# Values' products of two rounds in one visit of TensorE, and the sums of an attention divided anew between POOL and VectorE

## The chip, the cores and the metric

The kernel runs on one core of one Trainium2 chip. The metric is the device time of one execution in microseconds (us). TensorE is PE in the profile, with its weight loads as PEld; VectorE is DVE, ScalarE is ACT, GpSimd is POOL, SyncE is SP. A granted clock of 1.00 is TensorE at 2.4 GHz, its other level is 1.2 GHz.

## What is computed

Four blocks follow each other, each behind a layer norm and with a residual: a small state-space model, a feed-forward with quantized weights, an attention and a feed-forward with a mixture of low-rank parts. The change touches the third alone:

```python
q = jnp.dot(x, Wq).reshape(b, t, H, HD).transpose(0, 2, 1, 3)         # b 2, t 1024, H 32, HD 32
kv = jnp.dot(x, Wkv).reshape(b, t, G, 2, HD).transpose(2, 3, 0, 1, 4)  # G 8, four heads share k and v
scores = jnp.einsum('bhqd,bhkd->bhqk', q, k)
scores = jnp.where(causal[None, None], -jnp.inf, scores)
weights = jax.nn.softmax(scores * (1.0 / HD ** 0.5), axis=-1)
ctx = jnp.einsum('bhqk,bhkd->bhqd', weights, v)
return jnp.dot(ctx, Wo) + bo
```

All is float32. Where a plain matmul would not be exact enough, a factor is split into a high part (rounded to fp32r) and a low part (the rest), and three matmuls take the place of one.

## The kernel before

The attention is class `StageC`. Its loop has 16 **groups** `o` (two batches, eight sets of four heads `g` that share keys and values). A group has 12 **rounds** `r` (`ROUNDS`): rounds 0 to 3 are the first half of the queries (512 of them) against key blocks 0 to 3, rounds 4 to 11 the second half against key blocks 0 to 7. Rounds 0 to 3 and 8 to 11 touch the diagonal: they need a mask and have 512, 384, 256 and 128 columns; rounds 4 to 7 have 512. A round has four **slots**, one per head, so a group has 48 slots `s`, and `S = 48 * o + s` numbers them all. Each engine runs its own program over the same slots, and they meet in semaphores only.

**PE** (`pe`). Each slot has a score (`pe_score`, L2003: keys of one block against the queries of one head, into one of three PSUM banks) and one piece of the row maxima of the group ahead (`pe_amax`, L1985, in a ring of three other banks that `pe_turn` hands out). Many slots have a step of the projection of later query weights (`pe_job`, L1961 to L1963, three matmuls; in an ordinary group in even slots 2 to 16 and 32 to 46, so slots 18 to 31 have none). In slot 1 of a round (`g == 1`) comes a **visit** with the values' products (`pe_pv`, L2018) of the round two before: four heads side by side on 32 columns of the array each, two instructions per head, so eight matmuls in a row of the timeline. They accumulate in bank 5 over a half, and a half begins only when the half before has been copied out. `pe_sum` (L2044) makes the softmax denominators from the running sum `S` with a matrix of ones: at s == 5 for the second half of the group before, at s == 20 for the first half. In the groups `BY_ROUND` (4, 5, 14, 15) the first half's denominators are made round by round from the exponentials (`pe_sums`, L2034) inside the visit. `pe_mrow` transposes the maxima at s == 38.

**ACT** (`act_exp`, L2172). One exp per slot, from the score's bank into `P`, a ring of three rounds (`R % 3`, with R the round's number over all groups). The first head of round R waits until the products of round R - 3 are done, and the heads wait until the sums have read that buffer. ACT also casts the weights' high parts (`act_w4`, L2106) and the queries (`act_job`, L2130), and copies out the denominators and products of a half (`act_evac`, L2180 and L2185, at s == 6 and s == 22). In each slot the denominators' copy comes ahead of the exp, the products' copy behind it.

**DVE** (`dve`). One maximum per slot (`dve_amax`, L2323 and L2327), the low part of the queries (`dve_job`, L2312), the low parts of the next query weights in four pieces (`low_w4`, L2256), reciprocals, and in slots 23 to 26 the pair sums of rounds 4 and 5, one head each (`dve_pair`, L2269). At the end of the stage (`LAST`) it makes the running sums of groups 14 and 15 (`dve_last`, L2283).

**POOL** (`pool`). For each round, behind its last exp: the mask (`affine_select`, L2414), a multiplication of a finished half by its reciprocals (`pool_mul`, L2392, in rounds 0 and 4), and the running sum over rounds in `S` (round 1 in four instructions at L2431 and L2432, the others L2435; round 6 in two halves, L2408 and L2410). By the table `POOL_W` it also makes the low parts of a query weight in two places where the key weights' projection has crowded the slots: in round 8 of group 4 and in round 9 of group 8.

The order of work is written out by hand in the tables `JOBS`, `POOL_W`, `LAST`, `BY_ROUND` and in the fixed slots of each engine's loop. A semaphore that counts adds (`adds`, `psum_s`) tells how far `S` is.

## Time and profile before

| | |
|---|---|
| median of 3 runs | 2193.08 us (2185.26, 2194.05, 2193.08) |
| the profiled execution | 2189.54 us, span 2187.7 us, granted clock 0.969 |
| PE, DVE, ACT, POOL busy over the span | 2030.2, 1423.0, 946.4, 1003.7 us |
| attention: first score to last products | 957.7 to 1719 us |

The attention's groups take about 46.5 us each where nothing special happens (groups 1, 2, 7, 11, 12). "Busy" is the time in which an engine had an instruction under way; matmuls overlap, so 0.39 us for 512 columns is the life of one, and the distance of the starts is what it costs. A row of the windows view gives the stretch and its length, then the busy time (and number of instructions) of PE, the weight loads, DVE, ACT and POOL, the granted clock, the DMA engines' busy share and GB/s. A row of a timeline gives the start, the length, the engine, line, operation, result and operands, and how many such instructions it joins. An idle time in brackets names what ended it, by the semaphore that came last in the profile.

### The profile page before, as it was taken

Reading aid. Unit: us, or ns where it says so; the run is one execution under the profiler, and the core shown is the slowest. Engines: PE = TensorE matmul, PEld = TensorE weight load, DVE = VectorE, ACT = ScalarE, POOL = GpSimd, SP = SyncE. Lnnn points to the kernel's source line nnn. Section 1 sums busy time; section 2 is a strip of 40 time slices with the busy share of each in tenths; the row PEclk is TensorE's granted clock in tenths of the full one; section 3 lists DMA queues with packets and bytes.
Section 4 is the critical chain, followed back from the end, with each engine's and each line's share of the span. In section 5 each row is a group of like instructions: output and inputs, shape, how many; then the busy total and the mean of one; then the engine's idle time right before and its main releaser. Section 6 shows DMA issues by size and latency. Waiting matters only on the chain.

```text
span 2187.7 us, 30701 instructions
## 1 busy us (share of the span) xinstructions
PE 2030.2 (93%) x10444; PEld 1451.2 (66%) x10444; DVE 1423.0 (65%) x3290; ACT 946.4 (43%) x1979; POOL 1003.7 (46%) x866
## 2 busy tenths in 40 slices
PE   5889986999999989889999999999988999999998
PEld 4654545788888879755566555555554687888887
DVE  6877667677777762386765677567668577654433
ACT  5645685233333333135554555455555433332311
POOL 1444586544444430028875587667883133220000
PEclk9989998999999999999999999999997999999999
DMA  5400376122222147422223722323223375554332
GB/s 185 177 3 7 113 239 224 48 77 78 77 78 78 68 173 275 106 54 64 61 73 103 205 71 74 86 62 83 61 70 123 98 245 175 179 166 149 135 121 101
DMA packets 146475, 249.65 MB, mean 114 GB/s; under 512 B 27166, under 2 KB 77214, under 8 KB 146192
## 3 DMA queue, kind: packets, MB, share of 16 engines
q1 hardware_dynamic: 135312, 227.77, 32.8%
q10 hardware_dynamic: 11008, 19.93, 2.9%
q8 instruction: 83, 1.36, 0.3%
q14 instruction: 72, 0.59, 0.1%
HBM read 139.89 MB, written 76.02 MB: 99 GB/s over the span
## 4 chain that ended last, share of the span: by engine, by line
PE 60%; POOL 11%; DVE 9%; issue 3%; DMA 3%; ACT 2%; ACTq 1%; SPq 1%; DVEq 0%; POOLq 0%
POOL c_S L2435 7%; PE PS L2643 5%; PE PS L2644 5%; PE PS L2647 5%; PE PS L1130 3%; PE PS L1129 3%; PE PS L1128 3%; PE PS L2003 3%; PE PS L2018 3%; PE PS L1985 3%; PE PS L1178 2%; DVE PS L2327 2%; PE PS L1179 2%; PE PS L1180 2%; PE PS L1961 2%
## 5 line engine op out<-in xcount | busy, mean ns | idle before, releaser
L2172 ACT ACTIVATE c_P<-PS 128x512 f32<-128x512 f32 (+3 forms) x768 | 357.4, 494 | 320.6 <-PE PS L2003 301.4
L1985 PE MATMUL PS<-c_K,c_Q 96*128 96x512 f32 (+3 forms) x768 | 276.9, 371 | 21.3 <-DVE cst L2327 13.3
L2003 PE MATMUL PS<-c_Q,c_K 97*128 97x512 f32 (+3 forms) x768 | 282.5, 381 | 5.6 <-DMA c_Q<-c_mT 2.9
L2435 POOL TENSOR_TENSOR c_S<-c_S,c_P 128x2048 f32<-128x2048 f32 (+3 forms) x94 | 272.5, 2899 | 8.6 <-ACT c_P L2172 0.2
L2003 PEld LDWEIGHTS PS<-c_Q,c_K 97*128 97x128 f32 x768 | 147.8, 195 | 172.6 <-ACT c_P L2172 97.2
L2323 DVE TENSOR_REDUCE cst<-PS 128x1 f32<-128x512 f32 x256 | 175.9, 687 | 91.8 <-PE PS L1985 91.1
L213 POOL TENSOR_TENSOR maskw<-maskw,mhalf 128x1 f32<-128x1 f32 x64 | 37.1, 580 | 364.3 <-DVE maskw L171 351.9
L1985 PEld LDWEIGHTS PS<-c_K,c_Q 96*128 96x128 f32 x768 | 150.2, 196 | 77.0 <-DVE cst L2327 36.2
L2018 PE MATMUL PS<-c_P,c_V 128*32 128x512 f32 (+3 forms) x1536 | 168.5, 511 | 14.5 <-ACT c_P L2172 8.7
L2327 DVE CUSTOM_DVE_ANT_0 PS<-PS,maskw,cst 128x128 f32<-128x128 f32 (+3 forms) x256 | 142.9, 558 | 59.2 <-PE PS L1985 42.9
L2327 DVE CUSTOM_DVE_ANT_0 PS<-PS,maskw 128x128 f32<-128x128 f32 (+3 forms) x256 | 126.4, 504 | 62.6 <-PE PS L1985 60.5
L1274 ACT ACTIVATE b_g<-PS 128x460 f32<-128x460 f32 x96 | 53.0, 552 | 259.1 <-PE PS L1150 122.4
L1388 DVE SCALAR_TENSOR_TENSOR b_pr<-b_g,b_a 128x460 f32<-128x460 f32 x192 | 157.1, 854 | 1.7
L2414 POOL TENSOR_SCALAR_AFFINE_SELECT c_P<-c_P 128x512 f32<-128x512 f32 x128 | 83.0, 648 | 159.5 <-ACT c_P L2172 159.4
L1486 POOL TENSOR_TENSOR b_gp<-b_g 128x230 f32<-128x230 f32 x96 | 84.8, 883 | 152.1 <-DVE b_g L1373 152.1
L1128 PE MATMUL PS<-b_w13h,b_xsh 128*128 128x460 f32 (+1 forms) x384 | 148.1, 386 | 5.9 <-DVE b_xsl L1359 5.9
L2643 PE MATMUL PS<-c_xth,d_xh 128*128 128x512 f32 x376 | 147.7, 393 | 0.0
L2644 PE MATMUL PS<-c_xtl,d_xh 128*128 128x512 f32 x376 | 146.5, 390 | 0.0
L1130 PE MATMUL PS<-b_w13h,b_xsl 128*128 128x460 f32 (+1 forms) x384 | 143.8, 374 | 0.0
L1129 PE MATMUL PS<-b_w13l,b_xsh 128*128 128x460 f32 (+1 forms) x384 | 143.7, 374 | 0.0
L1961 PE MATMUL PS<-c_xth,c_wh 128*128 128x512 f32 x304 | 125.2, 412 | 5.5 <-POOL c_wl L2256 2.3
L1962 PE MATMUL PS<-c_xtl,c_wh 128*128 128x512 f32 x304 | 121.3, 399 | 0.0
(300 smaller groups left out, 4748.8 us busy)
## 6 DMA issues: line engine op xcount, KB each, us to landing
a_xin<-in_x SPq DMA_DIRECT2D x32, 512.0 KB, 4.4
d_x<-scr SPq DMA_DIRECT2D x32, 512.0 KB, 4.8
c_Q<-c_qh SPq DMA_DIRECT2D x240, 64.0 KB, 2.0
scr<-a_xin SPq DMA_DIRECT2D x16, 512.0 KB, 5.7
b_xn<-scr SPq DMA_DIRECT2D x16, 512.0 KB, 5.6
b_x<-scr SPq DMA_DIRECT2D x16, 512.0 KB, 4.8
scr<-b_x SPq DMA_DIRECT2D x16, 512.0 KB, 2.6
scr<-b_y SPq DMA_DIRECT2D x16, 512.0 KB, 3.0
```

Of the source, the lines that this page charges most:

```text
L1128: e.matmul(o, self.xsh[:, par, i, :], wh[:, v, i, :], start=i == 0 and not late, stop=False, skip_group_check=True)
L1129: e.matmul(o, self.xsh[:, par, i, :], wl[:, v, i, :], start=False, stop=False, skip_group_check=True)
L1130: m = e.matmul(o, self.xsl[:, par, i, :], wh[:, v, i, :], start=False, stop=i == 1 and bool(late), skip_group_check=True)
L1985: e.matmul(bank[:, 0:hi - lo], self.Q4[0:96, 4 * (o % 3) + g, 128 * t:128 * t + 128], self.K4[0:96, HEADS[o % 8], lo:hi], start=True, stop ...
L2003: e.matmul(self.k.bank(i % 3)[:, 0:hi - lo], self.K4[0:97, HEADS[o % 8], 128 * kt:128 * kt + 128], self.Q4[0:97, 4 * (o % 3) + g, lo:hi], ...
L2018: m = e.matmul(k.bank(5)[32 * g:32 * g + 32, lo - 512 * half:512], self.V[:, kt, o // 8, HEADS[o % 8], :], P[:, g, 0:hi - lo], start=kt == ...
L2172: e.activation(self.P[:, R % 3, g, 0:hi - lo], self.k.bank(i % 3)[:, 0:hi - lo], ACT.Exp, scale=SCALE).then_inc(self.exp_s.s, 1)
L2323: e.tensor_reduce(m, r, AX, ALU.max).then_inc(self.mx_s.s, 1)
L2327: e.tensor_tensor_reduce(out=r, in0=r, in1=self.maskw[:, 512 - n:512], scale=1.0, scalar=m if lo > 0 else -3.0e38, op0=ADD, op1=ALU.max, a ...
L2435: e.tensor_tensor(S[:, :, 512 - n:512], S[:, :, 512 - n:512], P[:, :, 0:n], ADD).then_inc(self.psum_s.s, 1)
L2643: e.matmul(o, h, wh[:, c, cols], start=c == 0, stop=False)
L2644: e.matmul(o, h, wl[:, c, cols], start=False, stop=False)
```

## The change

It has five parts, all in `StageC`.

1. In twelve groups (all but `SINGLE`: 5, 8, 14, 15) the values' products of rounds R - 1 and R run in one visit, in slot 1 of each odd round, and even rounds have no visit. The bank for the denominators by round (group 4) is taken at s == 13.
2. The denominators of the first half move from slot 20 to slot 21, behind the products; ACT copies them out behind the exp of slot 22, not ahead of it.
3. The low parts of the query weights go from DVE (slots 18 to 21) to POOL, round 4, in groups 1, 2, 3, 6, 7, 10, 11 and 12. In POOL's order they now stand behind the multiplication.
4. The pair sums of rounds 4 and 5: DVE makes heads 0 and 1 (slots 23 and 24), POOL heads 2 and 3 in one add in round 5.
5. Round 7 (`BOTH`): POOL adds heads 0 and 1, DVE heads 2 and 3 in slots 35 and 36 (not in groups 14 and 15). POOL's add of round 8 waits for DVE's.

```diff
+SINGLE = (5, 8, 14, 15)
-POOL_W = {(4, 8): JOB[7] + 1, (8, 9): JOB[11] + 1}
+POOL_W = {(4, 8): JOB[7] + 1, (8, 9): JOB[11] + 1} | {(o, 4): JOB[o + 3] + 1 for o in (1, 2, 3, 6, 7, 10, 11, 12)}
+BOTH = 7
...
-                if g == 1 and S > 8:
-                    self.pe_pv(e, *divmod(S // 4 - 2, 12))
+                R = S // 4 - 2
+                if g == 1 and R >= 0:
+                    if R // 12 in SINGLE:
+                        self.pe_pv(e, *divmod(R, 12))
+                    elif r % 2:
+                        self.pe_pv(e, *divmod(R - 1, 12))
+                        self.pe_pv(e, *divmod(R, 12))
                 if s == 5 and o > 0:
                     self.pe_sum(e, 2 * o - 1)
-                if s == 20 and o not in BY_ROUND:
+                if s == 21 and o not in BY_ROUND:
                     self.pe_sum(e, 2 * o)
...
             elif r3 in (4, 5):
-                e.wait_ge(*self.pair_s(4 * o3 + g + 1))
+                if g < 2:
+                    e.wait_ge(*self.pair_s(2 * o3 + g + 1))
+                elif g == 2:
+                    e.wait_ge(*self.pairp_s(o3 + 1))
...
+            elif r3 == BOTH and o3 < 15 and g == 2:
+                e.wait_ge(*self.both_s(2 * o3 + 2))
...
+                self.act_exp(e, o, r, g)
                 if s == 22:
                     self.act_evac(e, 2 * o, 1)
-                self.act_exp(e, o, r, g)
...
+    def dve_both(self, e, o, g):
+
+        e.wait_ge(*self.exp_s(48 * o + 4 * BOTH + g + 1))
+        e.wait_ge(*self.psum_s(self.adds(o, BOTH - 1)))
+        e.tensor_tensor(self.S[:, g, :], self.S[:, g, :], self.P[:, (12 * o + BOTH) % 3, g, :], ADD).then_inc(self.both_s.s, 1)
...
-                if 23 <= s < 27:
+                if 23 <= s < 25:
                     self.dve_pair(e, o, s - 23)
+                if s in (35, 36) and (o, BOTH) not in LAST and o < 15:
+                    self.dve_both(e, o, s - 33)
...
-                    e.wait_ge(*self.pair_s(4 * o + 4))
+                    e.wait_ge(*self.pair_s(2 * o + 2))
                     e.wait_ge(*self.exp_s(48 * o + 4 * r + 2))
                     e.tensor_tensor(S[:, 0:2, :], S[:, 0:2, :], P[:, 0:2, :], ADD)
+                    e.wait_ge(*self.pairp_s(o + 1))
...
+                if o > 0 and r in (0, 4):
+                    self.pool_mul(e, 2 * o - (2 if r == 0 else 1))
                 if (o, r) in POOL_W:
                     for q in range(4):
                         self.low_w4(e, POOL_W[o, r], q)
-                if o > 0 and r in (0, 4):
-                    self.pool_mul(e, 2 * o - (2 if r == 0 else 1))
+                if r == 5:
+                    e.wait_ge(*self.summed(2 * o - (o in BY_ROUND)))
+                    e.tensor_tensor(S[:, 2:4, :], self.P[:, (12 * o + 4) % 3, 2:4, :], P[:, 2:4, :], ADD).then_inc(self.pairp_s.s, 1)
...
                 e.wait_ge(*self.psum_s(self.adds(o, r - 1)))
-                e.tensor_tensor(S[:, :, 512 - n:512], S[:, :, 512 - n:512], P[:, :, 0:n], ADD).then_inc(self.psum_s.s, 1)
+                if r == BOTH + 1:
+                    e.wait_ge(*self.both_s(2 * o + 2))
+                gs = slice(0, 2 if r == BOTH else 4)
+                e.tensor_tensor(S[:, gs, 512 - n:512], S[:, gs, 512 - n:512], P[:, gs, 0:n], ADD).then_inc(self.psum_s.s, 1)
```

## Rows read from the trace of the kernel before

**Rows 1.** Busy time of the engines in the stretch of group 7, windows view.

```profile
1295.00:1342.00 47.00, 44.67 (x261) 27.27 (x261) 33.24 (x93) 26.49 (x61) 36.91 (x24) 1.00 0.27 69
```

**Rows 2.** Chain of waits over the same stretch, by engine, tile and line.

```profile
by line: POOL c_S L2435 42.1%; POOL c_S L2408 5.1%; POOL c_P L2414 5.1%; POOL c_S L2410 5.0%; DVE PS L2327 4.9%; PE PS L1985 4.8%; issue 4.7%; PE PS L2003 4.6%; DVE c_S L2269 4.2%; DVE cst L2323 3.8%; PE PS L2018 3.8%; PE PS L1961 3.1%; PE 
```

**Rows 3.** POOL's timeline from slot 20 of group 7 to slot 6 of group 8.

```profile
1315.33 1.34 POOL L2392 TENSOR_TENSOR c_cH<-c_cH,c_cS 128x512 f32<-128x512 f32 x1 [0.83 <-ACT c_P L2172]
1323.84 2.39 POOL L2408 TENSOR_TENSOR c_S<-c_S,c_P 128x1024 f32<-128x1024 f32 x1 [7.17 <-DVE c_S L2269]
...
1328.72 4.59 POOL L2435 TENSOR_TENSOR c_S<-c_S,c_P 128x2048 f32<-128x2048 f32 x1
...
1333.98 4.59 POOL L2435 TENSOR_TENSOR c_S<-c_S,c_P 128x2048 f32<-128x2048 f32 x1
...
1342.65 0.63 POOL L2414 TENSOR_SCALAR_AFFINE_SELECT c_P<-c_P 128x512 f32<-128x512 f32 x1
...
1346.43 1.28 POOL L2435 TENSOR_TENSOR c_S<-c_S,c_P 128x512 f32<-128x512 f32 x1
```

**Rows 4.** PE's timeline: slots 1, 5 and 45 of group 7.

```profile
1296.97 0.64 PE L2018 MATMUL PS<-c_P,c_V 128*32 128x256 f32 x8 [1.04 <-ACT c_P L2172]
...
1301.30 1.07 PE L2044 MATMUL PS<-c_S,cst 128*32 128x512 f32 x8 [0.22 <-POOL c_S L2435]
...
1339.30 0.85 PE L2018 MATMUL PS<-c_P,c_V 128*32 128x384 f32 x8 [0.24 <-POOL c_P L2414]
```

**Rows 5.** PE's timeline: slots 16, 17, 18, 20 and 32 of group 7.

```profile
1311.21 0.39 PE L2003 MATMUL PS<-c_Q,c_K 97*128 97x512 f32 x1
...
1312.37 0.40 PE L2003 MATMUL PS<-c_Q,c_K 97*128 97x512 f32 x1
1312.60 0.22 PE L1985 MATMUL PS<-c_K,c_Q 96*128 96x128 f32 x1
1312.76 0.64 PE L2018 MATMUL PS<-c_P,c_V 128*32 128x256 f32 x8
...
1313.67 0.40 PE L1985 MATMUL PS<-c_K,c_Q 96*128 96x512 f32 x1
...
1315.34 1.06 PE L2044 MATMUL PS<-c_S,cst 128*32 128x512 f32 x8 [0.45 <-DVE cst L2323]
...
1325.39 0.40 PE L2003 MATMUL PS<-c_Q,c_K 97*128 97x512 f32 x1
```

**Rows 6.** PE's timeline: products and denominators in one visit, group 4.

```profile
1149.78 1.06 PE L2018 MATMUL PS<-c_P,c_V 128*32 128x512 f32 x8
1150.66 1.04 PE L2034 MATMUL PS<-c_P,cst 128*32 128x512 f32 x8
```

**Rows 7.** ACT's timeline: exps of slots 19 and 23 to 25.

```profile
1314.65 0.60 ACT L2172 ACTIVATE c_P<-PS 128x512 f32<-128x512 f32 x1
...
1319.10 1.61 ACT L2172 ACTIVATE c_P<-PS 128x512 f32<-128x512 f32 x3
```

**Rows 8.** VectorE's timeline: two subtractions of low parts and a pair sum.

```profile
1315.11 0.41 DVE L2256 TENSOR_TENSOR c_wl<-c_raw,c_wh 128x256 fp32r<-128x256 f32 x1
...
1315.85 1.10 DVE L2256 TENSOR_TENSOR c_wl<-c_raw,c_wh 128x256 fp32r<-128x256 f32 x1
...
1320.18 0.69 DVE L2269 TENSOR_TENSOR c_S<-c_P 128x512 f32<-128x512 f32 x1
```

**Rows 9.** POOL's timeline: subtractions of low parts in group 4.

```profile
1184.29 2.79 POOL L2256 TENSOR_TENSOR c_wl<-c_raw,c_wh 128x256 fp32r<-128x256 f32 x4
```

**Rows 10.** POOL's timeline: a mask in group 14, while VectorE adds.

```profile
1679.52 0.98 POOL L2414 TENSOR_SCALAR_AFFINE_SELECT c_P<-c_P 128x512 f32<-128x512 f32 x1 [1.26 <-ACT c_P L2172]
```

**Rows 11.** Waits of attention: us in total, times, longest.

```profile
PE PS L1961 <- POOL c_wl L2256: 2.3, 2, 1.3
```

**Rows 12.** Windows view, slots 41 to 45 of group 13.

```profile
1630.00:1635.00 5.00, 3.67 (x16) 2.20 (x16) 2.47 (x6) 1.21 (x5) 5.00 (x2) 0.59 0.42 125
```

More of the change, by code:

```diff
@@ L1614, in __init__ @@
          self.whi_s, self.wlo_s, self.amax_s, self.mx_s, self.mtr_s, self.mtc_s, self.score_s, self.exp_s, self.diag_s,
-         self.pair_s, self.psum_s, self.pv_s, self.sum_s, self.evv_s, self.evs_s, self.rec_s, self.mul_s, self.wo_s) = k.sigs(
-            "c_", "given xtr xhi xlo vmm vcp qmm qhi qlo whi wlo amax mx mtr mtc score exp diag pair psum pv sum evv evs rec mul wo")
+         self.pair_s, self.psum_s, self.pv_s, self.sum_s, self.evv_s, self.evs_s, self.rec_s, self.mul_s, self.wo_s, self.both_s, self.pairp_s) = k.sigs(
+            "c_", "given xtr xhi xlo vmm vcp qmm qhi qlo whi wlo amax mx mtr mtc score exp diag pair psum pv sum evv evs rec mul wo both pairp")
         self.xld = [Sig(k, "c_x", 16, s, n) for s, n in ((before.ldc, 6), (before.ldb, 1), (before.lda, 1), (before.ld2, 6))]
@@ L1662, in tables @@
                     keeps.append(turn(o, 50))
-                if o in BY_ROUND and s == 9:
+                if o in BY_ROUND and s == (9 if o in SINGLE else 13):
                     kept = turn(o, 49)
@@ L1666, in tables @@
                     keeps.append(kept)
-                if o not in BY_ROUND and s == 20:
+                if o not in BY_ROUND and s == 21:
                     keeps.append(turn(o, 49))
@@ L2281, in dve_last @@
         else:
-            e.wait_ge(*(self.pair_s(60 + g + 1) if (o, r) == (15, 6) else self.dsum_s(n - 1, g)))
+            e.wait_ge(*((self.pair_s(30 + g + 1) if g < 2 else self.pairp_s(16)) if (o, r) == (15, 6) else self.dsum_s(n - 1, g)))
         e.tensor_tensor(self.S[:, g, cols], self.S[:, g, cols], self.P[:, (12 * o + r) % 3, g, 0:hi - lo], ADD
```

## The prediction

> **What bounds the kernel now.** I read the windows first, then the chain of waits, then the timelines of one attention group. In group 7 PE is busy 44.67 of 47 us, at the full 2.4 GHz, but POOL is busy 36.91 of 47 us as well [rows 1]. The chain over the same stretch lies on POOL's running sum for more than half of its length [rows 2]. The timeline of POOL shows how: from slot 20 on it waits 7.17 us for VectorE's last pair sum, and then it never stops, from 1323.84 to the end of the last add of the group at 1347.71 [rows 3]. PE runs into the tail of it: at slot 1 of each group the values' products wait 1.04 us for the mask of round 10, which stands behind an add on POOL (the trace names ACT), at slot 5 the denominators wait another 0.22 us for POOL's last add, and at slot 45 a mask costs 0.24 us [rows 4]. The first two come back in groups 2, 3, 7, 8, 11, 12 and 13 and in group 1. A third stall stands at slot 20, where the denominators of the first half wait 0.45 us for a PSUM bank [rows 5]. So the period of a group is one loop: denominators at slot 5 (1301.30), slot 16 (1311.21, 9.9 later), exps of round 5 and pair sums (12.6), POOL's chain (23.9), denominators at slot 5 of the next group (0.1 later): 46.5.
>
> **What the change does, part by part.** I write P16 for the start of slot 16.
>
> Visits. Twelve groups go from 12 visits with values' products to 6: 72 fewer. A visit costs more than its streaming. From the product at 1312.60 to the one at 1313.67 pass 1.07 us [rows 5]. In it lie 128 columns (0.06), a score (0.23, the spacing of 512 columns by 1312.37 to 1312.60) and products of 256 columns. Two sets of 512 columns in one visit start 0.88 us apart [rows 6], so 256 columns stream in 0.44. The rest, 0.3 us, is what entering and leaving costs. Bounds: 0 (if all of it belonged to the streaming) and 0.35. I take 0.3, the row that shows a visit. The denominators' move from slot 20 to 21 makes them share a visit too, and their bank has then been read, so 0.3 and 0.45 go, twelve times.
>
> Slots 16 to 31 take 14.18 us now [rows 5]. Without the stalls (some 2.0, the ones shown and smaller ones for VectorE) and with three visits fewer (0.9), PE would need 11.2. But ACT has work there: exps at 0.5 us each (three in 1.61 us, the last 0.6 long), two evacuations, a cast and four weight casts [rows 7]. I followed it: the exp of slot 23 ends 8.7 us after P16 (now 8.5), the next come every 0.5, and the score of slot 29, which needs the exp of slot 26, cannot start before 10.2. Then come a double visit of 2.3 with its products and two slots of 0.9 together: 13.4. Gain 0.8 of the 3.0 that PE alone would give.
>
> Late exps. In an odd round the first exp writes the buffer of three rounds before, whose products now run only in slot 1 of that round: it starts about 1.5 us later. PE has the second set (0.98), a score and a maximum (0.57) before it asks for that exp, and 0.7 more where the slot has query steps. The exp is 0.6 long and its start lags the end of the products by some 0.2. So 1.55 covers 0.8, and nothing waits. Cost zero; if the cover were one set shorter, 0.3 to 0.4 per visit.
>
> The weights' low parts. In 8 groups four subtractions leave VectorE (0.41 long each [rows 8]) and go to POOL in round 4 (four in 2.79 us [rows 9]). They fall into POOL's idle 7.17 us: the multiplication starts at P16 + 4.1 [rows 3], ends at 5.4, the subtractions end at 8.2. The one whose casts come last is ready at 6.7. The next load of weights on SP waits for them and is no later than now.
>
> Pair sums. Two of four leave VectorE (0.69 long each [rows 8]). POOL makes both in one add of 1024 columns, 2.4 us, and needs the exp of slot 23. That can start at P16 + 8.7. Then come the two adds of round 6 (4.9) as now.
>
> Round 7. POOL adds 1024 columns instead of 2048: 2.45 instead of 4.6. VectorE adds the other two heads in slots 35 and 36, and POOL's add of round 8 now waits for them.
>
> Loop for a group with all parts, ideal: pair sum at 8.7, + 2.45, + 4.9, + 2.45, + 1.15 (mask of round 8 and the wait for VectorE), + 13.7 (start of the add of round 8 to the end of round 11's, 1333.98 to 1347.71 [rows 3]) = 33.35. Now it is 12.63 + 23.87 = 36.5. Denominators 0.08 later, then 9.9 to the next P16, less one visit: 9.6. Period 43.0 against 46.5, a gain of 3.5. PE's own loop would be 42.6, so POOL still sets it.
>
> **A price that speaks against the change.** VectorE and POOL disturb each other. The subtraction on VectorE that took 0.41 us at 1315.11 took 1.10 at 1315.85 [rows 8]: it lay under POOL's multiplication (1315.33 to 1316.67 [rows 3]) and ended 0.28 after it. The other way round, a mask of 0.63 us took 0.98 where VectorE streamed sums [rows 10]. Neither starves the other, the one that waits gets the next turn. The change puts four additions of VectorE into stretches where POOL works. The first pair sum of VectorE (wanted at 7.05) meets the subtractions, the second too, and POOL's pair sum then starts at 9.4 instead of 8.7. In round 7 VectorE's two adds are wanted at 17.3 and 18.2, while POOL adds until 19; they end at 19.7 and 21 with the mask in between, and round 8 starts 1.9 instead of 1.15 after round 7. Loop: 9.4 + 2.45 + 4.9 + 2.45 + 1.9 + 13.7 = 34.8; period 44.5; gain 2.0 per group. I take this one, since the 1.10 us comes back in seven groups, and longer in two more. The Trainium skill (SBUF — State Buffer, Who interferes with whom) says that an instruction of VectorE with two SBUF inputs and one of GpSimd that reads SBUF exclude each other for the whole instruction. The trace agrees (1.10 against 0.41). Without such a rule the gain would be the 3.5 above.
>
> **The sum.** Nine loops (from groups 0, 1, 2, 3, 6, 7, 10, 11, 12) at 2.0: 18. Group 13 has no query steps after slot 31, so POOL alone sets it: in a stretch of it POOL is busy 5.00 of 5 us and PE 3.67 [rows 12]. By the same loop, with the start at 8.7 (nothing is subtracted in it), round 8 begins at 20.4 instead of 22.8; with two visits: 3. Groups 6 and 10, whose first slots PE bounds, one visit each: 0.6. Group 0 waits at slot 20 for POOL's add of round 3, and one slot of cover comes ahead of that: 1. Group 4: four visits and POOL's earlier turn on key weights, whose two stalls are 2.3 us [rows 11]: 2.4. Group 8: 1.7 (the other of these stalls and slot 20's). Group 5: two pair sums off a late VectorE, 1.3. Group 9: the same and visits, 2.1. Groups 14 and 15: 1.3. Together 31.4. The profiled execution took 2189.54 us, so it would take 2158; the median of the runs shown is 3.5 higher, so I forecast 2162.
>
> **Rivals.**
> A. No meetings of weight: 3.5 instead of 2.0 in nine loops (13.5), some 1.5 more in group 13: 2147. For it: VectorE has slack beside query steps. Against it: the 1.10. Chance 0.2.
> B. POOL's chain hardly starts earlier. If POOL's pair sum gets in ahead of VectorE's second one, that one ends 3 us later, and round 6 needs both; if also VectorE's adds of round 7 come behind the mask, round 8 starts 1 us later still. The gain per loop falls to about 0.5: 2175. It decides at 9.4 after P16. Chance 0.22.
> C. Slower: the late exps. If the exps of odd rounds come so late that PE waits 0.7 us in each of the 72 double visits, this costs 50 and eats the 31: 2212. It needs 0.44 us per visit to turn the sign, that is an exp that starts 1.2 us after its products, or products whose completion shows only after the second set. Against it: exps now follow products and scores within 0.5 us. Chance 0.07.
> D. The change doesn't do what its first part says: the 0.3 us belong to the streaming of these products and stay when two visits become one. POOL's loop then gains 1.7 instead of 2.0 (nine times), and the groups that PE bounds some 4 less in all: 2168. Chance 0.06.
> A fifth thing moves any of these: after the long stalls of group 13 the granted clock fell to 0.59 of full (a mean over both levels, 2.4 and 1.2 GHz) [rows 12]. Stalls that go may save such stretches, a new stall of that size may add one: 3 us either way.
>
> **How the numbers follow.** My forecast has 0.45, with its own range 2153 to 2171. A measurement of this kernel can tell about 0.5% (11 us) from no change. Faster by more, below 2182: forecast, A, D and half of B: 0.82. Within 0.5%: the other half of B, 0.11. Slower: C, 0.07. The range of 8 in 10 runs from 2142 (A, with the clock's part) to 2184 (B with a few more).
>
> **What would show it.** In the changed profile: the products on PE in rows of 16 and 6 visits a group; the exp of slot 28 about 1.5 us later than its score and no wait of PE for exps at slot 31; POOL's pair sum about 9.4 us after P16 and round 8's add about 21; VectorE's sums 1 to 2.4 us long where POOL works; the stall at slot 1 gone and one of 1 to 2 us before the denominators at slot 5; a period near 44.5 us in groups 1, 2, 7, 11, 12. I am wrong if POOL idles between rounds 5 and 11, if PE waits for ACT in the odd rounds, or if the period is below 43.

## The result, and the profile after

The changed kernel takes 2209.09 us (median of 6 runs, 2205.97 to 2211.80) where the kernel before takes 2191.63 on the same chips (6 runs, 2184.57 to 2194.05): the ratio is 1.0087, 95% interval 1.0073 to 1.0100. It is slower, by 0.9%, and 47 us above the forecast. The profiled execution took 2211.80 us with a span of 2209.9 and a mean granted clock of 0.957 (before 0.969). One of the seven executions of `mixed_pairs` below took 6020.9 us, and its ratio leaves that one out.

The page of the changed kernel, groups by line (busy us, mean ns | idle time of the engine before them, and what ended most of it):

```profile
PE 2034.4 (92%) x10444; PEld 1462.5 (66%) x10444; DVE 1438.2 (65%) x3254; ACT 939.1 (42%) x1979; POOL 1037.0 (47%) x914
...
L1991 PE MATMUL PS<-c_K,c_Q 96*128 96x512 f32 (+3 forms) x768 | 280.0, 375 | 49.7 <-DVE cst L2349 37.1
...
L2466 POOL TENSOR_TENSOR c_S<-c_S,c_P 128x1024 f32<-128x1024 f32 (+3 forms) x94 | 242.0, 2575 | 54.4 <-ACT c_P L2188 28.6
...
L2024 PE MATMUL PS<-c_P,c_V 128*32 128x512 f32 (+3 forms) x1536 | 170.3, 552 | 2.1 <-POOL c_P L2439 1.2
```

The same groups of the kernel before:

```profile
L1985 PE MATMUL PS<-c_K,c_Q 96*128 96x512 f32 (+3 forms) x768 | 276.9, 371 | 21.3 <-DVE cst L2327 13.3
...
L2435 POOL TENSOR_TENSOR c_S<-c_S,c_P 128x2048 f32<-128x2048 f32 (+3 forms) x94 | 272.5, 2899 | 8.6 <-ACT c_P L2172 0.2
...
L2018 PE MATMUL PS<-c_P,c_V 128*32 128x512 f32 (+3 forms) x1536 | 168.5, 511 | 14.5 <-ACT c_P L2172 8.7
```

Part of what was aimed at happened: POOL's running-sum line is 30 us less busy, and TensorE's wait before the products fell from 14.5 to 2.1. POOL as a whole is 33 us busier (1037.0, 1003.7 before). That it idles 54.4 us before these adds instead of 8.6 is not slack won: 28.6 of them are waits for exponentials, and with the loss removed (pool_after_dve, below) 23.7 are left. What took the place of the old waits is in the first row: TensorE waits 49.7 us before row maxima instead of 21.3, and 37.1 of it (13.3 before) is for VectorE's earlier maxima.

One ordinary group shows where. Timelines of the changed kernel, group 7, slots 21 to 31; POOL:

```profile
1327.86 2.82 POOL L2272 TENSOR_TENSOR c_wl<-c_raw,c_wh 128x256 fp32r<-128x256 f32 x4
1331.05 2.41 POOL L2448 TENSOR_TENSOR c_S<-c_P 128x1024 f32<-128x1024 f32 x1 [0.37 <-ACT c_P L2188]
1334.09 2.37 POOL L2432 TENSOR_TENSOR c_S<-c_S,c_P 128x1024 f32<-128x1024 f32 x1 [0.63 <-DVE c_S L2285]
```

VectorE:

```profile
1330.50 0.72 DVE L2285 TENSOR_TENSOR c_S<-c_P 128x512 f32<-128x512 f32 x1
...
1331.36 2.65 DVE L2285 TENSOR_TENSOR c_S<-c_P 128x512 f32<-128x512 f32 x1
1333.93 0.42 DVE L2349 CUSTOM_DVE_ANT_0 PS<-PS,maskw 128x256 f32<-128x256 f32 x1
```

TensorE:

```profile
1332.08 0.41 PE L2009 MATMUL PS<-c_Q,c_K 97*128 97x512 f32 x1
1334.46 0.50 PE L1991 MATMUL PS<-c_K,c_Q 96*128 96x512 f32 x1 [1.97 <-DVE cst L2349]
...
1335.24 3.56 PE L2024 MATMUL PS<-c_P,c_V 128*32 128x512 f32 x16
1338.73 0.52 PE L2009 MATMUL PS<-c_Q,c_K 97*128 97x512 f32 x1
```

Windows over it (stretch and its length, busy time of PE, weight loads, DVE, ACT, POOL, then the granted clock):

```profile
1330.00:1333.00 3.00, 2.19 (x8) 1.19 (x8) 3.00 (x6) 2.92 (x6) 2.63 (x2) 1.00 0.11 30
1333.00:1336.00 3.00, 1.54 (x8) 0.64 (x11) 3.00 (x8) 0.00 (x0) 2.37 (x2) 0.90 0.99 276
1336.00:1340.00 4.00, 4.00 (x22) 1.52 (x15) 1.02 (x4) 1.80 (x4) 2.77 (x2) 0.65 0.44 100
```

The reader sees a chain of four. POOL's new pair add begins at 1331.05. VectorE's second pair sum begins 0.31 us later and lasts 2.65 us, where the first took 0.72 ([rows 8]: 0.69); it ends 0.55 us after POOL's add. The maxima queued behind it are late, and TensorE stands 1.97 us at slot 28, with no query step in these slots to fill the gap. Then the granted clock falls to a mean of 0.65, a mixture of both levels, and the double visit of slot 29 takes 3.56 us (1.92 in pool_after_dve, below, where it runs at 2.4 GHz).

The groups' lengths, from the starts of the scores of slots 0, 16, 32 and 48 in each trace, group 7:

```
                   slots 0-15  16-31  32-47   whole
before                 16.13   14.18  16.17   46.48
after                  14.57   17.52  15.23   47.32
```

Two of the three parts gained (1.6 and 0.9 us); slots 16 to 31 lost 3.3. The stall at slot 28 (27 in three groups) stands in 13 of the 16 groups, all but 4, 8 and 15, with 1.4 to 2.2 us each. In 12 of them the mean granted clock over the 4 us behind the stall is 0.50 to 0.71; in group 14 it stays at 1.00. From first score to last products the attention took 761.3 us before and 783.7 after: the whole difference of the two spans (22.2) lies there. Its mean clock is 0.93 (0.97 before).

### The profile page after: what moved, and what is told of

Same layout as the page of the kernel before. It is cut to its first block and busy times, and to the rows that moved or that the text cites. A ratio compares the mean times of both kernels' runs of the same rounds, so it can differ in the third digit from the quotient of the medians.

```text
span 2209.9 us, 30720 instructions
## 1 busy us (share of the span) xinstructions
PE 2034.4 (92%) x10444; PEld 1462.5 (66%) x10444; DVE 1438.2 (65%) x3254; ACT 939.1 (42%) x1979; POOL 1037.0 (47%) x914
## 5 line engine op out<-in xcount | busy, mean ns | idle before, releaser
L2188 ACT ACTIVATE c_P<-PS 128x512 f32<-128x512 f32 (+3 forms) x768 | 351.1, 497 | 362.6 <-PE PS L2009 186.7
L1991 PE MATMUL PS<-c_K,c_Q 96*128 96x512 f32 (+3 forms) x768 | 280.0, 375 | 49.7 <-DVE cst L2349 37.1
L2466 POOL TENSOR_TENSOR c_S<-c_S,c_P 128x1024 f32<-128x1024 f32 (+3 forms) x94 | 242.0, 2575 | 54.4 <-ACT c_P L2188 28.6
L2349 DVE CUSTOM_DVE_ANT_0 PS<-PS,maskw 128x128 f32<-128x128 f32 (+3 forms) x256 | 123.6, 504 | 42.6 <-PE PS L1991 41.4
```

Of the source, the lines that this page charges most:

```text
L1991: e.matmul(bank[:, 0:hi - lo], self.Q4[0:96, 4 * (o % 3) + g, 128 * t:128 * t + 128], self.K4[0:96, HEADS[o % 8], lo:hi], start=True, stop ...
L2188: e.activation(self.P[:, R % 3, g, 0:hi - lo], self.k.bank(i % 3)[:, 0:hi - lo], ACT.Exp, scale=SCALE).then_inc(self.exp_s.s, 1)
L2349: e.tensor_tensor_reduce(out=r, in0=r, in1=self.maskw[:, 512 - n:512], scale=1.0, scalar=m if lo > 0 else -3.0e38, op0=ADD, op1=ALU.max, a ...
L2466: e.tensor_tensor(S[:, gs, 512 - n:512], S[:, gs, 512 - n:512], P[:, gs, 0:n], ADD).then_inc(self.psum_s.s, 1)
```

## The experiments

Theory M: the meeting of the two pair sums, through VectorE's late maxima and the clock, is the loss. Rivals: late exponentials of the double visits (the prediction's C), or another part of the change. All edits are to the changed kernel. Ratios are to the kernel before, run alongside (medians 2188.6 to 2191.4).

**pool_after_dve**, one wait more, so that POOL's pair add follows both of VectorE's:

```diff
                 if r == 5:
+                    e.wait_ge(*self.pair_s(2 * o + 2))
```

> One wait more: POOL's pair sum of round 5 waits for VectorE's second pair sum, so the two no longer meet. Theory 1 (the collision: VectorE's second pair sum, 2.65 us instead of 0.7 because it began 0.3 us behind POOL's, holds back the maxima, PE waits 1.95 us at slot 28 and then runs the double visit at the low clock): slots 16 to 31 of group 7 fall from 17.5 to 13.5 to 14 us, the stall at slot 28 is gone, the double visit of slot 29 takes 1.9 instead of 3.6 us, and the whole falls by 30 to 38 us, to about 2171 to 2179. Theory 2 (late exps: the double visits starve PE of exps in the slots without query steps): the stall moves to ACT, slots 16 to 31 stay above 16.5, total 2200 or more. Theory 3 (the low parts on POOL delay its pair sum and so the chain): less than 10 us gained.

Measured 2177.13 us, 0.9941 (0.9919 to 0.9963). The profiled execution took 2183.58, the longest of its four. POOL's, VectorE's and TensorE's timelines of it, group 7, and a row of its page:

```profile
1318.20 2.38 POOL L2449 TENSOR_TENSOR c_S<-c_P 128x1024 f32<-128x1024 f32 x1 [1.50 <-ACT c_P L2188]
...
1329.56 4.63 POOL L2467 TENSOR_TENSOR c_S<-c_S,c_P 128x2048 f32<-128x2048 f32 x1 [0.72 <-DVE c_S L2291]
```

```profile
1316.57 0.69 DVE L2285 TENSOR_TENSOR c_S<-c_P 128x512 f32<-128x512 f32 x1
1317.38 0.69 DVE L2285 TENSOR_TENSOR c_S<-c_P 128x512 f32<-128x512 f32 x1
1326.17 2.17 DVE L2291 TENSOR_TENSOR c_S<-c_S,c_P 128x512 f32<-128x512 f32 x1
```

```profile
1318.52 0.50 PE L1991 MATMUL PS<-c_K,c_Q 96*128 96x512 f32 x1
...
1319.30 1.92 PE L2024 MATMUL PS<-c_P,c_V 128*32 128x512 f32 x16
```

```profile
L1991 PE MATMUL PS<-c_K,c_Q 96*128 96x512 f32 (+3 forms) x768 | 280.7, 376 | 27.6 <-DVE cst L2349 13.5
```

One wait turns the loss into a gain: 1.0087 less 0.9941 is 1.5%, 32 us. The two pair sums take 0.69 each, TensorE's wait for maxima on the page is 13.5 us instead of 37.1, the stall at slot 28 is gone, and the mean clock over the attention is 0.96 instead of 0.93. The 23.6 us of that wait, and the halved clock behind it, stand against 28.4 us between the two profiled spans; how the 28.4 divide between the two is not measured. Together with the next run that settles M for the loss; it leaves 15 us to the forecast.

**pairs_on_dve**, part 4 undone: all four pair sums on VectorE again.

```diff
-                if 23 <= s < 25:
+                if 23 <= s < 27:
...
-                    e.tensor_tensor(S[:, 2:4, :], self.P[:, (12 * o + 4) % 3, 2:4, :], P[:, 2:4, :], ADD).then_inc(self.pairp_s.s, 1)
```

> Part 4 undone alone: all four pair sums on VectorE, in slots 23 to 26; visits, low parts and round 7 as changed. Theory 1: no collision in slots 24 to 27, VectorE has two additions more (1.2 us); slots 16 to 31 about 14 us; POOL's chain starts at 12 to 12.5 us after slot 16 and is 1 to 2 us shorter than before the change; total 2172 to 2185. Theory 2: stays above 2200, since the visits are as changed. Theory 3: above 2195, since the low parts are still on POOL.

Measured 2176.66 us, 0.9932 (0.9911 to 0.9954): the same as with the wait. So part 4 with its meeting was the whole of the loss, and without its meeting it is worth nothing that these runs can tell.

**single_visits**, part 1 undone, one round a visit (`SINGLE` holds all 16 groups).

> Part 1 undone alone: one visit per round in all groups; the sums and low parts as changed. Theory 1: the stall at slot 28 (1.95 us) stays, the exp of slot 28 no longer waits for it, the low clock hits a single visit; slots 16 to 31 about 16 to 17; 0 to 16 and 32 to 48 lose 0.6 each by the visits; total 2200 to 2215. Theory 2: slots 16 to 31 fall to 14 or less and the total to 2175 to 2190.

Measured 2204.91 us, 1.0063 (1.0040 to 1.0086). The second pair sum still takes 2.66 us in group 7 and TensorE still waits 1.50 at slot 28: the loss doesn't need the double visits.

**visits_only**, parts 3, 4 and 5 undone; only parts 1 and 2 are left.

> Parts 1 and 2 alone: double visits and the denominators at slot 21; pair sums, low parts and round 7 as in the kernel before. Theory 1: no collision. The visits save 0.3 us each where PE bounds, POOL's chain bounds the ordinary groups as before (period 46.2): total 2178 to 2190, slots 16 to 31 about 14.2. Theory 2: slots 16 to 31 above 16, total above 2205.

Measured 2189.30 us, 0.9996 (0.9984 to 1.0007). The ordinary group takes 46.15 us with a wait of 0.83 for POOL before the denominators at slot 5: POOL's loop still bounds, as the prediction read it, and visits alone gain nothing. Slots 16 to 31 of group 7 take 15.06 us, where about 14.2 was expected: a first sign that double visits cost something there.

**early_pairs**, VectorE's pair sums one slot earlier (`if 22 <= s < 24`, g = s - 22), to win the race without a wait.

> As changed, but VectorE's two pair sums one slot earlier, in slots 22 and 23: the second one then begins about 0.5 us ahead of POOL's pair sum instead of 0.3 us behind it, with no wait added. Theory 1 (the collision alone): VectorE's second pair sum 0.7 us long, no stall of 1.9 us at slot 28, no low clock behind it, POOL's pair sum no later than as changed; slots 16 to 31 of group 7 13.9 us or less, total 2170 to 2180, as with the added wait or a little below. If the added wait helped in another way than by keeping the two apart, this one stays near 2205.

Measured 2203.84 us, 1.0066 (1.0040 to 1.0092), a miss for what I had expected of it. But it holds both cases in one execution. VectorE's timeline of it, group 7 and then group 11:

```profile
1323.30 0.83 DVE L2285 TENSOR_TENSOR c_S<-c_P 128x512 f32<-128x512 f32 x1
...
1324.72 0.68 DVE L2285 TENSOR_TENSOR c_S<-c_P 128x512 f32<-128x512 f32 x1
```

```profile
1535.16 1.20 DVE L2285 TENSOR_TENSOR c_S<-c_P 128x512 f32<-128x512 f32 x1
...
1536.96 2.56 DVE L2285 TENSOR_TENSOR c_S<-c_P 128x512 f32<-128x512 f32 x1
```

In group 7 POOL's add begins at 1324.75, 0.03 behind VectorE's: that one takes 0.68, and POOL's takes 2.89 instead of 2.4. In group 11 POOL's begins at 1536.62, 0.34 ahead: VectorE's takes 2.56. Whoever starts first keeps the other out. Slots 16 to 31 take 15.39 us in group 7 and 17.73 in group 11. In group 11 the first pair sum (1.20) had been held by POOL's subtractions of low parts, so part 3 had pushed the second behind POOL's add. The other ordinary groups (1, 2, 3, 6, 10, 12) went as group 11, with TensorE waiting 2.0 to 2.3 us at slot 27, which is why the total missed. And group 7 itself took 15.39 where 13.9 or less was expected, without such a wait (its longest there is 0.39 us): the clock fell all the same. Windows over it:

```profile
1322.00:1325.00 3.00, 2.35 (x9) 1.47 (x10) 2.31 (x5) 3.00 (x7) 2.97 (x5) 1.00 0.00 0
1325.00:1329.00 4.00, 3.99 (x16) 2.06 (x19) 3.33 (x12) 1.62 (x4) 4.00 (x2) 0.61 0.67 179
```

**wait_single**, the wait and single visits in every group.

> With the wait that removes the collision, one visit per round in all groups (part 1 undone). What double visits are worth without the collision. My account: 0.3 us per visit, seen in full in slots 0 to 15 and 32 to 47 (0.6 each per group) unless POOL's chain fills it; late exps cost nothing: total 2183 to 2192, 6 to 15 above the kernel with the wait. If the late exps cost as much as the visits save: 2173 to 2181.

Measured 2176.96 us, 0.9944 (0.9919 to 0.9969): as with double visits, and not the 6 to 15 us above them of my account. By thirds, group 7: 15.30, 12.91 and 16.54 us against 14.56, 13.86 and 16.07. Double visits save 0.5 to 0.7 where query steps fill the slots (0.4 of the 0.7 are waits for POOL at slots 1 and 5 that only the single visits have), and lose 0.95 in slots 16 to 31. ACT's timeline there, with double visits (pool_after_dve):

```profile
1316.40 2.59 ACT L2188 ACTIVATE c_P<-PS 128x512 f32<-128x512 f32 x5
1320.48 2.79 ACT L2188 ACTIVATE c_P<-PS 128x512 f32<-128x512 f32 x5 [1.49 <-issue]
```

and with single ones (wait_single):

```profile
1312.68 2.06 ACT L2188 ACTIVATE c_P<-PS 128x512 f32<-128x512 f32 x4 [0.28 <-PE PS L2009]
1315.52 1.58 ACT L2188 ACTIVATE c_P<-PS 128x512 f32<-128x512 f32 x3 [0.78 <-PE PS L2009]
```

The exp of slot 28 waits for the products that a double visit puts off to slot 29. It starts at 1320.48, 2.32 us after its score (forecast 1.5); ACT idles 1.49 and has a row of five to make up.

**wait_low** (the wait, low parts back on VectorE: the added entries of `POOL_W` go) and **wait_noboth** (the wait, round 7 wholly on POOL: `BOTH = 99`) price parts 3 and 5.

> With the wait, the low parts of the query weights back on VectorE, slots 18 to 21 (part 3 undone). If VectorE is what bounds slots 16 to 31 (14.2 before, 13.9 with the wait), the 1.3 us of them come back in eight groups: total 2183 to 2190. If ACT bounds these slots, as in my working: no more than 3 us above 2177.

> With the wait, round 7 wholly on POOL again (part 5 undone). POOL's chain gets 2.2 us longer but loses the wait for VectorE and the meetings of slots 35 to 37 (VectorE's additions there 2.17 and 0.90 us long, PE 0.59 us idle at slot 36). My account: about 1 us more per ordinary group, seen as a stall before the denominators at slot 5: total 2183 to 2190. If the meetings cost as much as the shorter chain gives: 2174 to 2180.

Measured 2185.17 us, 0.9978 (0.9961 to 0.9995), and 2189.60 us, 1.0006 (0.9987 to 1.0025). Against 2177 part 3 is worth 8 us, though the two intervals overlap a little, and part 5 12. The 8 us are more than the 3 that were allowed if ACT alone bounds slots 16 to 31: with the low parts on VectorE those slots take 14.47 us in group 7 instead of 13.86, so ACT alone is not their bound. Without part 5 the wait at slot 5 for POOL is back (0.75 in group 7), so POOL's loop is where part 5 pays.

**mixed_visits**, the wait, single visits for rounds 2 to 5 and in groups 0 and 9; **mixed_pairs**, the same with all pair sums on VectorE.

```diff
-SINGLE = (5, 8, 14, 15)
+SINGLE = (0, 5, 8, 9, 14, 15)
...
-                    if R // 12 in SINGLE:
+                    if R // 12 in SINGLE or R % 12 in (2, 3, 4, 5):
```

> POOL's pair add waits for both of VectorE's, and the products of rounds 2 to 5 (slots 17 to 29, where no query steps stand) are made one round a visit again in every group, those of the other rounds two a visit; groups 0 and 9 one a visit throughout. Theory (a double visit saves its share where query steps lie between, slots 0 to 15 and 32 to 47, and costs through late exponentials where only ScalarE is short, slots 16 to 31): an ordinary group takes 14.6 + 12.9 + 15.9 = 43.4 us in place of 44.49 and 44.75; over nine groups 10 less, group 0 4 less and group 9 3 less than with the wait and all double visits: 2160, between 2155 and 2166. Rival (the loop with the wait is closed by POOL's chain, and what slots 16 to 31 gain comes back as a stall before the denominators at slot 5 or the products at slot 45): 2168 to 2177, with slots 0 to 15 or 32 to 47 longer by what was gained.

> The same mixed visits, with all four pair sums on VectorE (slots 23 to 26) instead of the wait. Theory: slots 16 to 31 are then bounded by VectorE rather than by ScalarE (14.42 with double visits), so the mixed visits gain less there, 0 to 0.6 a group; with groups 0 and 9, 2167 to 2172, above mixed_visits by some 7. Rival (ScalarE's late exponentials set those slots here too): about 2160, as mixed_visits.

Measured 2179.24 us, 0.9952 (0.9934 to 0.9970), and 2173.24 us, 0.9915 (0.9898 to 0.9931). The first missed its 2155 to 2166, and the second, expected some 7 us above the first, is 6 below. Their profiled executions, 2188.32 and 2184.10 us, lie 9 and 11 above the medians. The slots' times came out (14.56 and 12.91 us in group 12), but a new wait of 0.8 to 2.7 us stands at slot 36 in most ordinary groups, for which the trace mostly names no engine ("issue"). In group 11 VectorE's add of round 7 lay blocked beside it for 2.85 us, so I first took the same meeting at its second place for the cause.

**two_waits** and **two_waits_pairs**, that meeting removed as well.

```diff
-                if s in (35, 36) and (o, BOTH) not in LAST and o < 15:
-                    self.dve_both(e, o, s - 33)
+                if s == 35 and (o, BOTH) not in LAST and o < 15:
+                    self.dve_both(e, o, 2)
+                    self.dve_both(e, o, 3)
...
-                if r == BOTH + 1:
+                if r in (BOTH, BOTH + 1):
```

> The mixed visits with the wait, and the same cure at the second place where VectorE and POOL add at once: VectorE's two adds of round 7 stand together in slot 35, and POOL's own add of round 7 waits until both are done. Theory (a VectorE add that starts within POOL's is shut out until POOL's ends, and TensorE's gap of 1.3 to 2.5 us at slot 36 of mixed_visits is that): VectorE's adds take 0.7 us each, the gap at slot 36 falls under 0.5, slots 32 to 47 take 16.0 in place of 16.3 to 19.3, an ordinary group 43.4, and the time is 2156 to 2168. Price: POOL's round 8 add starts 0.5 to 1.5 us later, within what its loop has free. Rival 1 (POOL's loop has nothing free): the gap comes back as 0.5 to 1.5 us before the denominators at slot 5 or the products at slot 45, 2170 to 2180. Rival 2 (the gap at slot 36 has another cause): it stays, and so do 2179.

> The same second cure with all four pair sums on VectorE in place of the first wait: by the theory the gap at slot 36 (0.8 to 2.7 us in mixed_pairs) goes, 2155 to 2166; if POOL's loop is short it is hit less here, since POOL has no pair add but starts its chain at the same moment: within 5 us of two_waits. Rival 2: 2173 as mixed_pairs.

Measured 2192.21 us, 1.0016 (1.0003 to 1.0028), and 2191.93, 1.0018 (1.0004 to 1.0031): 13 and 19 us lost. VectorE's two adds took 1.29 together, and the wait at slot 36 stayed (1.94 us in group 11, 1.44 in group 7). So it was not that meeting (rival 2). And POOL had nothing to give: it now waits 1.6 us for VectorE in groups 7 and 11, and such waits come back at slots 1, 5 and 45 of other groups (rival 1) and above all in groups 4 and 8, where the key weights' low parts stand behind the adds: TensorE waits 4.58 us for them at slot 39 and 4.17 at slot 44 (in mixed_visits 0.88 at slot 39, and that for a maximum of VectorE, and 1.61 at slot 44).

TensorE's maximum at slot 36 is the first of group o + 2 and needs that group's queries in place. SP's timeline of mixed_visits, group 7:

```profile
1316.44 0.40 SPq L1745 DMA_DIRECT2D c_raw<-in_wk  x1
1316.95 0.52 SPq L1803 DMA_DIRECT2D c_Q<-c_qh  x1
...
1323.84 0.59 SPq L1803 DMA_DIRECT2D c_Q<-c_qh  x1
```

and TensorE's:

```profile
1325.93 0.30 PE L1991 MATMUL PS<-c_K,c_Q 96*128 96x128 f32 x1 [1.45 <-issue]
```

SP issues the load of the next weights when POOL's subtractions are done (1316.41), 8.6 us after slot 16; the twelve transfers of the queries' second half stand behind it, go out in 7.5 us, and the last is issued 2.09 us before TensorE goes on. That is a second bound, 18.1 us from slot 16 to the maximum of slot 36, and hidden while the slots between take that long. What the next three kernels change is only this order.

**load_mixed**, **load_pairs** and **load_double**: SP issues that load behind the placement; on mixed_visits, on mixed_pairs and on pool_after_dve.

```diff
-                for n, q in self.split_at.get(S, ()):
-                    if q == 3:
-                        self.sp_w(e, n + 2)
+                for back in (0, 2):
+                    for n, q in self.split_at.get(S - back, ()):
+                        if q == 3 and (S - back + 2 in self.place_at) == (back == 2):
+                            self.sp_w(e, n + 2)
```

> As mixed_visits (one wait, mixed visits), and in the ordinary groups SP issues the load of the next weights behind the second half of the queries' placement instead of ahead of it. Theory (the gap at slot 36 is the wait for that placement: SP stands at the load until POOL's subtractions are done, 8.5 us after slot 16, then issues twelve transfers at 0.63 us each, and the last lands as slot 36 begins): the placement starts over 5 us earlier, the gap at slot 36 goes (1.3 to 2.5 us in six groups, and the halved clock behind it in three), 2179 becomes 2158 to 2168. Rival (the gap is VectorE's blocked add of round 7, which takes 2.1 to 2.9 us there): VectorE's maxima are still late, a gap of 0.5 to 1.5 us moves to slots 37 to 39, and the time is 2170 to 2178.

> The same order of SP on mixed_pairs (all pair sums on VectorE, mixed visits). Theory: the gap at slot 36 goes, 2173 becomes 2155 to 2165. Rival: 2168 to 2174.

> The same order of SP with the wait and double visits everywhere, where the gap at slot 36 is 0.6 us in two ordinary groups and 2.2 us in group 5. Theory: the placement sets little here, 2171 to 2177 in place of 2177, so that load_mixed beats it by 5 or more: then the double visits of slots 17 to 31 are a loss. If load_mixed is no faster than this one, they are not, whatever the slots' own times say.

Measured 2172.72 us, 0.9928 (0.9906 to 0.9951); 2168.77 us, 0.9903 (0.9879 to 0.9926); and 2177.50 us, 0.9951 (0.9934 to 0.9967). SP's timeline of load_mixed, group 7, whose slot 16 starts at 1299.24:

```profile
1302.66 0.51 SPq L1803 DMA_DIRECT2D c_Q<-c_qh  x1
...
1309.55 0.59 SPq L1803 DMA_DIRECT2D c_Q<-c_qh  x1
1310.18 0.58 SPq L1745 DMA_DIRECT2D c_raw<-in_wk  x1
```

The placement starts 3.4 us after slot 16 instead of 9.1, and no ordinary group of the three kernels waits 0.4 us or more at slot 36, although VectorE's add of round 7 still takes 2.90 us in group 7. That shows the cause of the wait at slot 36. What its end is worth in the total is not shown: 6.5, 4.5 and 0 us, less than expected, and the intervals before and after overlap in all three. Slots 0 to 15 went back from 14.56 to 15.32, with 0.55 at slot 5 waiting for POOL's last add: POOL's loop is the bound again, at 44.5 us. And in group 5 a wait at slot 32 grew from 2.3 to 3.2 us in load_mixed and from 2.2 to 3.4 in load_double. load_mixed beats load_double by 4.8 us, about what was expected, but their intervals overlap.

load_pairs is the best version found: 21 us, 1.0%, below the kernel before and 40 below the changed one. In both pairs of kernels with mixed visits the one without POOL's pair add is ahead (by 6.0 and 4.0 us; the intervals of the second pair overlap).

By thirds, group 7 (12 for mixed_visits, the one group of it without the wait at slot 36), made as above:

```
                   slots 0-15  16-31  32-47   whole
pool_after_dve         14.56   13.86  16.07   44.49
pairs_on_dve           14.56   14.42  15.49   44.47
wait_single            15.30   12.91  16.54   44.75
mixed_visits, 12       14.56   12.91  16.26   43.73
load_mixed             15.32   12.91  16.27   44.50
load_double            14.58   13.88  15.52   43.98
```

## Why the prediction was wrong

**What failed: the price of a meeting.** The prediction had the right resource and the right pair of instructions, and its rival B even named this order of them. Two steps failed. First, "neither starves the other, the one that waits gets the next turn" rested on a subtraction of 0.41 us that took 1.10, under a POOL instruction of 1.34. What the traces show is that the later one waits for all of the earlier one, so the price grows with POOL's instruction: 2.65 us under one of 2.41. The Trainium skill (SBUF — State Buffer, Who interferes with whom) says that the ports which the two share are under an exclusive lock, and that the order of issue decides which of them is blocked. The trace agrees, with those numbers; the prediction cited the section and then priced by the 1.10. Second, the forecast put POOL's pair add at 9.4 us after slot 16 and VectorE's second sum ahead of it. POOL began at 8.9, VectorE 0.3 later. VectorE was the late one: its first sum was wanted at 7.05 and started at 8.35 (8.97 before the change), because the maxima ahead of it had waited for TensorE, not because of POOL. The prediction had named 9.4 as the point that decides, and the order fell on the other side of it.

**What was missing: who stands behind VectorE.** B was followed along POOL's chain only, which gave 2175. The instruction that was blocked on VectorE had the row maxima queued behind it, and TensorE waits for those in slots that have nothing else. Round 8's add did slide, to 23.5 us after slot 16 (22.8 before, 21.1 forecast, 21.3 once the wait was added). The larger price was 1.95 us of TensorE in most groups and then the halved clock. The side note that a stall may cost a clock stretch allowed 3 us for all of them.

**Late exponentials at zero.** They start 2.3 us after their score, not 1.5, and slots 17 to 31, which have no query steps, don't cover it: 0.95 us longer with double visits (13.86 against 12.91), though two visits fewer stand there. Rival C was right in its mechanism for those slots, and far off in its size (50 us). Group 0 (no query steps in its first slots: 13.6 us double, 10.6 single) and group 9 (24.6 against 20.3 in slots 16 to 31) lost as well, where gains of 1 and 2.1 us were forecast, but most of the loss in group 0 is the clock's. Windows over slots 0 to 15 of group 0, both with double visits, of pool_after_dve and then of early_pairs:

```profile
958.23:971.85 13.62, 12.59 (x49) 6.25 (x48) 9.83 (x31) 7.09 (x17) 8.49 (x8) 0.78 0.25 58
```

```profile
956.42:967.73 11.31, 10.09 (x50) 5.21 (x48) 9.57 (x31) 6.89 (x17) 6.18 (x8) 1.00 0.31 70
```

At the full clock the double visits cost 0.7 us there (10.6 with single ones), and the other 2.3 go with the lower clock. It stands in these slots in seven of the eight profiled executions with double visits in them (13.4 to 13.6 us) and in four of the nine with single ones (12.4 to 12.5). In group 9 slots 16 to 31 had a mean clock of 0.72 with double visits and 0.94 with single ones.

**The sum of 31.4.** With the meeting removed, from slot 16 of one group to slot 16 of the next, the nine loops gave 12.5 us instead of 18 (five of them 1.7 or 1.8; those that start in groups 0 and 6 only 0.4 and 0.6, with a mean clock of 0.76 and 0.89 in their slots 16 to 31). All the rest, 13.4 in the forecast, came to a loss of 5.8, since the attention as a whole took 754.6 us in that execution, 6.7 less than before: group 9 took 55.65 against 53.31, groups 5, 8, 14 and 15 stayed within 0.3 us, group 13 gave 0.9 of 3. That execution was 6.5 us above its kernel's median, so a part of this loss may be its own.

**"No later than now" for the load on SP.** It was issued 7.6 us after slot 16 before (1318.79, slot 16 at 1311.21 [rows 5]) and 8.6 after the change (1330.71, 1322.15): part 3 made it 1.0 later. That cost nothing in the changed kernel itself, but it is the start of the chain that held mixed_visits at slot 36. The prediction did not look at what stands behind the load in SP's queue.

**What held.** POOL's loop was the bound, and still is when only the visits change. The period forecast with all parts was 44.5; with the meeting removed group 7 takes 44.49 from score to score. Of the terms behind it these were met: 21.3 for round 8 (21.1), no wait at slot 1, and 0.3 us saved for the visit less (slots 8 to 15 of group 7, where nothing waits for POOL, take 7.40 us with single visits and 7.08 with double ones). Others were not, so that the agreement to 0.01 us is in part luck: slots 16 to 31 took 13.86 (13.4), and the stall of 1 to 2 us before the denominators at slot 5, which was to show that POOL alone sets the period, is 0.07 us behind group 7 and at most 0.6 in groups 1 to 13. TensorE's own loop, put at 42.6, takes about as long as POOL's in that group. POOL's idle time did take the low parts, worth 8 us, and VectorE's share of round 7 was worth 12.

## What to carry to other kernels

Where a VectorE instruction with two SBUF operands and a GpSimd one can start close together, price the worse order: VectorE loses the whole length of the GpSimd instruction, and so does everything queued behind it; then ask who waits for that queue, not only for the sum. If the order matters, write it as a wait on the engine that has slack, and check that it has: the same kind of wait gained 32 us at one place and cost 13 at another. And when a shortened stretch doesn't show in the total, look for a transfer that stands behind something unrelated in its queue.

## What the runs showed of the hardware that was not expected

- The exclusion is decided by tenths of a microsecond: 0.03 us ahead, VectorE's sum takes 0.68 us and POOL's add 2.89 (0.5 longer); 0.31 or 0.34 us behind, it takes 2.65 and 2.56. Even 0.03 behind, VectorE's add of round 7 takes 2.85 under one of POOL's of 2.34 (mixed_visits, group 11).
- A gap of 2 us on TensorE can cost nearly as much again by the granted clock, but not always. Behind the gap of 1.94 us in group 11 of two_waits (the visit after it takes 3.59 us) and that of 2.17 in group 10 of mixed_visits (3.89 for its slot, 2.24 in group 11), it was 0.69 and 0.68 over the next 4 us; behind a gap of 2.53 us in group 11 of mixed_visits and one of 2.22 in group 10 of two_waits it stayed at 1.00. The same gap of 1.97 us at slot 21 of group 8 was followed by 0.57 in the changed kernel and by 1.00 in pool_after_dve. Windows of two_waits, then of mixed_visits, both of group 11:

```profile
1536.00:1540.00 4.00, 3.76 (x18) 1.56 (x22) 1.12 (x6) 0.46 (x2) 3.62 (x3) 0.69 0.12 32
```

```profile
1536.00:1540.00 4.00, 4.00 (x29) 2.44 (x22) 2.07 (x9) 2.27 (x6) 3.60 (x1) 1.00 0.36 113
```

What makes the difference stays open. Nor is such a gap needed: in group 7 of early_pairs and in the first slots of group 0 the clock fell where TensorE waited for less than half a microsecond at a time.
